# States carried through DRAM with three transfers in place of sixteen, and the turning of halves put two steps later

## The chip, the cores and the metric

The kernel runs on one core of one Trainium2 chip, as one launch. The metric is the device time of that launch in microseconds (us): the median of three runs. One further execution was taken with the hardware profiler on; every row below is of it.

## The reference, cut to what matters

The input is 16 images of 192 channels by 32 x 32 positions (1024 tokens). Each image goes through three parts, each with a residual: a convolution-like mixing part, a windowed attention, and an expert layer (4 experts, top 2 per token). The change is in the mixing part, whose core is a linear recurrence along the rows and along the columns, in both directions, with a state of 16 numbers:

```python
def _ssm1d(x, a_logit, U, V, Win, bin_, Wg, bg, Wout, bout, Wskip, bskip, reverse):
    if reverse:
        x = x[:, ::-1]
    u = jnp.einsum('nld,sd->nls', x, Win) + bin_
    g = jax.nn.sigmoid(jnp.einsum('nld,sd->nls', x, Wg) + bg)
    a = jax.nn.sigmoid(a_logit)
    A = jnp.diag(a) + (U @ V.T).T
    gu = jnp.swapaxes(g * u, 0, 1)
    def step(h, gu_t):
        h = h @ A + gu_t
        return (h, h)
    _, hs = jax.lax.scan(step, h0, gu)
    ...
yr = _ssm1d(rows, *rp, False) + _ssm1d(rows, *rp, True)
yc = _ssm1d(cols, *cp, False) + _ssm1d(cols, *cp, True)
y = (yr + yc) * 0.25
...
return g * y + (1.0 - g) * x
```

The mixed tokens are then normalised and projected to queries, keys and values for the attention.

## The kernel before, in words

**Order of the whole.** While the experts of image i run, the mixing part of image i+1 is done in between, so that TensorE (PE) always has expert work to put into gaps. `experts(i)` goes through 4 blocks of 512 tokens in 6 chunks each, 24 chunks. A chunk n is `ffn1(n)` (5 matmuls into one PSUM bank), a GELU on ScalarE (ACT, `gelu`, L818), a split of the result into two halves of float16 on VectorE (DVE, `split`, L1057 and L1060), and two chunks later `ffn2(n-2)` on PE (L1528 to L1530). `ffn1(n)` waits for `gelu(n-2)`.

**Steps.** The side work is written as generators (`conv`, `tail`, `rest`, `dispatch`), one of each per engine, and each `yield from til(step_no, k)` says that what follows runs in step k+1. The list `STEPS` says how many steps each chunk makes: (a, b) is a steps between `ffn1` and `ffn2` and b steps after `ffn2`. That split counts on PE alone; ACT does `gelu(n)` and then all a+b steps of the chunk, DVE `split(n)` and then all a+b steps. Before the change chunks 0 to 15 have (1, 1), chunks 16 and 17 (2, 1), and chunks 18 to 23 (2, 2). One step is made ahead of chunk 0. Every engine works its own instructions in order, so an instruction that waits holds up all that stands behind it on that engine. There is no planner: the order is this list and the numbers given to `til`.

**The scan.** PE projects the normalised image (L1388); ACT takes a tanh of the gates (L772); DVE multiplies gates and inputs into `GU` in two halves (row kind L994, column kind L998), each of which adds to `gu_ready`. In `GU` the 16 states lie on 16 partitions and the 32 positions of a line along the free axis. The scan itself (L1404, 14 float32 matmuls on ready-made powers of the recurrence, shown as 28 passes) wants eight positions times 16 states on 128 partitions, in `GUP`. `input_moves` does this rearrangement: the SP queue issues 16 DMAs of 8 KB (L588, 8 for each kind), each from 16 partitions to 16 others. PE runs the scan in step 11 and waits there for all 16 (`gu_moved`). ACT copies the result into `HSP` (L779); `state_moves` brings it back with 16 more DMAs (L596), 8 into `HST` for the rows, which GpSimd (POOL) then permutes (`conv_states`, L687 and L688) and SP places (`state_place`, L600), and 8 straight into `XG` for the columns. The states are wanted in step 28, when the mixing of the eight token tiles (L1446 to L1454) begins. Between these moves the SP queue also loads the experts' weights (`expert`, L623) and tokens (`tokens`, L610).

**The turning of halves.** The eight tiles are mixed in steps 28 to 35; the last two in chunk 16. After a tile, DVE ends the residual (L1021, L1023) and takes statistics; after each four tiles POOL raises the variance to the power -1/2 (L678) and makes the shift (L697). ACT normalises four tiles (`first_norm(k)`, L851), DVE splits them into float16 halves (`first_halves(k)`, L1145 and L1146), and PE turns them (12 transposes, L1463; `xnr_ready` is the wait). When both halves are turned, ACT and DVE copy the windows (L490 to L494), and then PE projects them (`project`, L1487), 18 pieces, one in a step. In the numbers of `til`: `first_norm(1)` 36 on ACT, `first_halves(1)` 37 on DVE, turning 37 and 39 on PE, windows 41 and 42, projections 45; and, in `dispatch`, the prefix sums of the router 36 on PE (L1537), `positions` 38 and `schedule` 39 on DVE.

The lines of this order:

```python
STEPS = [(1, 1) if n < 16 else (2, 1) if n < 18 else (2, 2) for n in range(NSEL * HK)] + [(1, 1)]
...
def experts(i, *side):          # ACT
    step(side, STEPS_AHEAD)
    for n in range(blocks_of(i) * HK):
        gelu(i, *divmod(n, HK))
        step(side, sum(STEPS[n % len(STEPS)]))
```

Images 0 to 2 differ: image 0 is mixed before anything else, image 1 after the attention of image 0, with no experts beside it, and image 2 beside the single block of six chunks of image 1. The other 13 images (3 to 15) are mixed beside 24 chunks.

Of the kernel before, what the change touches and what calls it, by code (L numbers as in the profile page):

```python
# [6 lines left out]
F32 = mybir.dt.float32  # L7
# [44 lines left out]
    x_loaded=16, gn_channel=1, gn_mean=1, gn_spread=1, gn_var=1, gn_eps=1, gn_rstd=1, xg_ready=2, xs_ready=2,  # L52
    proj_done=1, tanh_done=1, gu_ready=2, gu_moved=16 * 2 * KP, scan_done=1, hs_copied=1, hs_rows_moved=16 * KP,
    hs_cols_moved=16 * KP, hs_permuted=1, hs_placed=16, xgT_done=NP, h1_read=NP, mixln_eps=1, mixln_rstd=1, h1_pre=1,
    h1_gelu=1, h1T_done=1, h1T_copied=1, mix_done=NT, mix_tanh=NT, mixed=NT,
# [18 lines left out]
def hybrid_kernel(nc, x, proj_w, y_wa, y_wb, y_scale, eye, gavg, cavg, norm_w, norm_b, g1_wT, g1_b, g2_wT, bias_row,  # L74
                  scan_v, scan_u, scan_a, wqkv, wo, bq, bk, bv, mask, w1, w2, b1, gate_w, gate_b, before, after,
                  consts, tri, out, powers, slots, weights):
    ctx = ExitStack()
    with ctx:
# [333 lines left out]
        def at(name, i, k):  # L412

            return i * PER[name] + k
# [46 lines left out]
        def til(count, k):  # L461

            while count[0] < k:
                count[0] += 1
                yield
# [15 lines left out]
        STEPS_AHEAD = 1  # L481
        STEPS = [(1, 1) if n < 16 else (2, 1) if n < 18 else (2, 2) for n in range(NSEL * HK)] + [(1, 1)]
        GATE_AT, MIX_AT = (15, 16, 18, 19), 27
# [98 lines left out]
        def _(sp):  # L582
            def input_moves(i):
                for kind in range(2):
                    sp.wait_ge(s["gu_ready"], at("gu_ready", i, kind + 1))
                    src = GU[32 * kind:32 * kind + S, :].rearrange("s (c i n) -> s c i n", c=KC, i=KP)
                    for k in range(KP):
                        sp.dma_start(GUP[S * k:S * k + S, kind, :, :], src[:, :, k, :]).then_inc(s["gu_moved"], 16)  # L588

            def state_moves(i):  # L590
                sp.wait_ge(s["hs_copied"], at("hs_copied", i, 1))
                for kind, moved in ((0, s["hs_rows_moved"]), (1, s["hs_cols_moved"])):
                    dst = (HST.rearrange("s (c i) n -> s c i n", i=KP) if kind == 0 else
                           XG[97:113, 1, :].rearrange("s (c i n) -> s c i n", c=KC, i=KP))
                    for k in range(KP):
                        sp.dma_start(dst[:, :, k, :], HSP[S * k:S * k + S, kind, :, :]).then_inc(moved, 16)  # L596

# [77 lines left out]
        def _(pool):  # L675
# [8 lines left out]
            def conv_states(i):  # L684
                pool.wait_ge(s["hs_rows_moved"], at("hs_rows_moved", i, 16 * KP))
                pool.wait_ge(s["xs_ready"], at("xs_ready", i, 2))
                pool.tensor_tensor(PSPARE, PSPARE, PSPARE, ALU.mult)  # L687
                pool.tensor_copy(HST2.rearrange("s (h w) -> s h w", h=GH), HST.rearrange("s w h -> s h w")  # L688
                                 ).then_inc(s["hs_permuted"], 1)
# [72 lines left out]
        def _(act):  # L762
# [12 lines left out]
            def conv(i):  # L775
                step_no = [4 if first(i) else 0]
                yield from til(step_no, 10)
                act.wait_ge(s["scan_done"], at("scan_done", i, 1))
                act.activation(HSP[:].rearrange("p a b c -> p (a b c)"), PSUM[:, 3, 0:2 * KC * GW], ACT.Copy  # L779
                               ).then_inc(s["hs_copied"], 1)  # L780
                yield from til(step_no, 22)
                act.wait_ge(s["h1_pre"], at("h1_pre", i, 1))
                act.activation(H1[:], H1[:], ACT.Gelu).then_inc(s["h1_gelu"], 1)
                yield from til(step_no, 25)
                act.wait_ge(s["h1T_done"], at("h1T_done", i, 1))
                act.activation(H1T[:].rearrange("p a b -> p (a b)"), PSUM[:, 0, 0:256], ACT.Copy
                               ).then_inc(s["h1T_copied"], 1)
                for t in range(NT):
                    yield from til(step_no, MIX_AT + t)
                    act.wait_ge(s["mix_done"], at("mix_done", i, t + 1))  # L790
                    if t >= 2:
                        act.wait_ge(s["mixed"], at("mixed", i, t - 1))
                    act.activation(TM[:, (t % 2) * C:(t % 2 + 1) * C], PSUM[:, t % 2, 0:C], ACT.Tanh, scale=0.5
                                   ).then_inc(s["mix_tanh"], 1)
                    if t == 6:
                        first_norm(i, 0)
                yield from til(step_no, 36)
                first_norm(i, 1)
                yield from til(step_no, 41)
                act.wait_ge(s["xn1T_done"], at("xn1T_done", i, 1))  # L800
                windows(act.copy, 0, 0)
                windows(act.copy, 0, 1)
                yield from til(step_no, 42)
                windows(act.copy, 2, 0)
                windows(act.copy, 2, 1).then_inc(s["win_act"], 1)
                yield from til(step_no, 45)
                for n in range(PIECES):
                    if n % 2 == 0:
                        act.wait_ge(s["piece_done"], at("piece_done", i, n + 1))
                        evacuate_piece(act, n, s["piece_act"])  # L810
                    yield
# [108 lines left out]
        def _(dve):  # L920
# [69 lines left out]
            def conv(i):  # L990
# [46 lines left out]
                first_halves(i, 1)  # L1037
                yield from til(step_no, 41)
                dve.wait_ge(s["xn1T_done"], at("xn1T_done", i, 1))
                dve.memset(XW[:, :, 0, 0:PAD - 1], 0.0)  # L1040
                dve.memset(XW[:, :, NB - 1, T - LAST_KEY:KW], 0.0)
                windows(dve.tensor_copy, 1, 0)
                yield from til(step_no, 42)
                windows(dve.tensor_copy, 1, 1).then_inc(s["win_dve"], 1)
                yield from til(step_no, 45)
                for n in range(PIECES):
# [327 lines left out]
        def _(pe):  # L1374
# [17 lines left out]
            def conv(i):  # L1392
                step_no = [4 if first(i) else 0]
                yield from til(step_no, 10)
                pe.wait_ge(s["gu_ready"], at("gu_ready", i, 2))
                pe.wait_ge(s["gu_moved"], at("gu_moved", i, 16 * 2 * KP))
                if not first(i):
# [35 lines left out]
                for t in range(NT):  # L1433
                    yield from til(step_no, MIX_AT + t)
                    if t == 0:
                        pe.wait_ge(s["h1T_copied"], at("h1T_copied", i, 1))
                        pe.wait_ge(s["hs_copied"], at("hs_copied", i, 1))
                        pe.wait_ge(s["hs_cols_moved"], at("hs_cols_moved", i, 16 * KP))
                        pe.wait_ge(s["hs_placed"], at("hs_placed", i, 16))
# [17 lines left out]
                for k in range(2):  # L1457
                    yield from til(step_no, 37 + 2 * k)
                    pe.wait_ge(s["mixed"], at("mixed", i, NT))
# [5 lines left out]
                    if k == 1:  # L1465
                        mm.then_inc(s["xn1T_done"], 1)
                yield from til(step_no, 45)
                pe.wait_ge(s["win_act"], at("win_act", i, 1))
# [336 lines left out]
```

## Time and profile before

| what | us |
|---|---|
| median of three runs | 3132.28 |
| lowest and highest of them | 3127.65, 3137.54 |
| the profiled execution, its own time | 3132.16 |
| its span, first to last instruction | 3130.4 |

The profiled execution lies within the three runs, so its rows can be held against the median. Times in the rows are microseconds from the start of the span. In a timeline each row is a start, a length, the engine, the line of the kernel, the operation with output and input, how many instructions the row merges, and, in brackets, how long the engine sat idle before it and who ended that. "SPq" and "ACTq" are DMA issues on a queue. PEclk is the clock that TensorE was granted, as a share of full speed.

### The profile page before, as it was taken

To read this page: it belongs to the slowest core of one execution; us is meant where nothing else is said; L and a number is where in the kernel's file an instruction comes from. 1 tells how busy PE (TensorE), PEld (TensorE's weight loads), DVE (VectorE), ACT (ScalarE), POOL (GpSimd) and SP (SyncE) were. 2 spreads that over 40 slices of the span, in tenths; PEclk is the share of its full clock that TensorE was granted. 3 is DMA by queue.
4 is the path that set the end of the run, shared out by engine and by line. 5 is a ranking of instruction groups with operands and counts; after the bars stand their busy time and mean duration, and the time that the engine had idled before them with its cause. 6 is when DMAs were issued, how large, how long until landed. Compare 5 with 4: busy or idle time off the path is not lost. (4 is left out here: it accounts for less than half of the span.)

```text
span 3130.4 us, 50074 instructions
## 1 busy us (share of the span) xinstructions
PE 2541.2 (81%) x18177; PEld 1957.0 (63%) x18177; DVE 1945.5 (62%) x5667; ACT 989.8 (32%) x2341; POOL 919.4 (29%) x704
## 2 busy tenths in 40 slices
PE   1367787888888888888888898888888898888597
PEld 0256565666767666675767676676767676676365
DVE  4465655666666656666666657666666666666364
ACT  0031323243342424233342424233342424243122
POOL 0001203051332415051332414151332415051544
PEclk9786878898998989898998989898998989899799
DMA  2520203123242414123242514223242414223565
GB/s 43 118 88 15 58 15 99 36 67 77 67 98 62 110 43 116 49 56 88 66 99 62 110 36 120 52 61 83 65 100 62 110 39 117 53 58 98 132 154 113
DMA packets 272437, 242.20 MB, mean 77 GB/s; under 512 B 208989, under 2 KB 250175, under 8 KB 261569
## 3 DMA queue, kind: packets, MB, share of 16 engines
q1 hardware_dynamic: 211456, 147.61, 17.8%
q0 software_dynamic: 50880, 52.59, 9.5%
q10 hardware_dynamic: 9856, 38.80, 4.0%
q8 instruction: 146, 2.39, 0.3%
q14 instruction: 99, 0.80, 0.1%
HBM read 133.73 MB, written 73.59 MB: 66 GB/s over the span
## 5 line engine op out<-in xcount | busy, mean ns | idle before, releaser
L1510 PE MATMUL PSUM<-XT,WB 128*128 128x512 f16 x2010 | 546.6, 408 | 29.1 <-DMA META<-slots 27.3
L818 ACT ACTIVATE HF<-PSUM,WB 128x512 f32<-128x512 f32 x402 | 277.2, 690 | 692.2 <-PE PSUM L1510 691.4
L678 POOL TENSOR_TENSOR TR<-TV,MHALF 128x4 f32<-128x4 f32 x64 | 75.8, 1185 | 1182.9 <-DVE TV L932 1182.9
L726 POOL DMA_INDIRECT out_dram<-Y,META x228 | 355.7, 1560 | 208.2 <-issue 207.9
L1057 DVE TENSOR_SCALAR HHI<-HF 128x512 f16<-128x512 f32 x402 | 175.6, 437 | 387.1 <-ACT HF L818 385.2
L841 ACT ACTIVATE PSPT<-PSUM,NMX 94x126 f32<-94x126 f32 x1056 | 286.9, 362 | 406.7 <-PE PSUM L1569 288.2
L1528 PE MATMUL PSUM<-WB,HHI 128*128 128x192 f16 x1608 | 413.7, 257 | 0.2
L1529 PE MATMUL PSUM<-WB,HHI 128*128 128x192 f16 x1608 | 412.7, 257 | 0.0
L1530 PE MATMUL PSUM<-WB,HLO 128*128 128x192 f16 x1608 | 412.3, 256 | 0.0
L1510 PEld LDWEIGHTS PSUM<-XT,WB 128*128 128x128 f16 x2010 | 206.8, 107 | 210.5 <-issue 50.8
L1579 PE MATMUL PSUM<-VW,PSPT 126*94 126x33 f32 x2112 | 218.2, 255 | 111.0 <-DVE PSPT L1095 110.9
L1557 PE MATMUL PSUM<-KBD,QT 128*94 128x378 f32 x704 | 296.4, 504 | 14.5 <-ACT PSPT L841 12.8
L711 POOL DMA_INDIRECT slots<-XROW,IDX x256 | 255.3, 997 | 167.4 <-DVE IDX L1253 88.7
L1060 DVE SCALAR_TENSOR_TENSOR HLO<-HF,HHI 128x512 f16<-128x512 f32 x402 | 279.3, 695 | 13.8
L1579 PEld LDWEIGHTS PSUM<-VW,PSPT 126*94 126x94 f32 x2112 | 198.1, 169 | 143.0 <-DVE PSPT L1095 143.0
L1111 DVE TENSOR_REDUCE NMX<-PSUM 94x3 f32<-94x378 f32 x352 | 184.7, 542 | 74.3 <-PE PSUM L1560 72.2
L1487 PE MATMUL PSUM<-OSX,WQKV 128*96 128x372 f16 (+3 forms) x960 | 188.0, 343 | 31.7 <-issue 22.3
L1529 PEld LDWEIGHTS PSUM<-WB,HHI 128*128 128x128 f16 x1608 | 165.3, 103 | 34.6 <-issue 12.2
L1528 PEld LDWEIGHTS PSUM<-WB,HHI 128*128 128x128 f16 x1608 | 168.6, 105 | 27.4 <-issue 7.5
L1404 PE MATMUL PSUM<-GUP,SCAN 128*128 128x64 f32 (+3 forms) x448 | 98.5, 415 | 92.6 <-issue 75.7
L1487 PEld LDWEIGHTS PSUM<-OSX,WQKV 128*96 128x96 f16 x960 | 117.2, 126 | 85.3 <-issue 24.9
L1530 PEld LDWEIGHTS PSUM<-WB,HLO 128*128 128x128 f16 x1608 | 164.9, 103 | 1.4
(270 smaller groups left out, 4393.0 us busy)
## 6 DMA issues: line engine op xcount, KB each, us to landing
WB<-weights SPq DMA_DIRECT2D x67, 1600.0 KB, 7.2
XR<-in_x ACTq DMA_DIRECT2D x16, 768.0 KB, 5.6
out_dram<-X ACTq DMA_DIRECT2D x32, 384.0 KB, 2.4
weights<-WB ACTq DMA_DIRECT2D x4, 1600.0 KB, 6.6
GUP<-TGU SPq DMA_DIRECT2D x256, 8.0 KB, 1.8
slots<-XROW,IDX POOLq DMA_INDIRECT x256, 2.4
out_dram<-Y,META POOLq DMA_INDIRECT x228
HF<-in_w ACTq DMA_DIRECT2D x6, 384.0 KB, 6.3
```

The lines of the kernel that those rows point to most:

```text
L711: pool.indirect_dma_start(slots[:, :].bitcast(I32), bass.IndirectOffsetOnAxis(IDX[:, k, t:t + 1], 0), XROW[:, t, :].bitcast(I32), None, bo ...
L726: pool.indirect_dma_start(out[:, :], bass.IndirectOffsetOnAxis(row, 0), Y[:, wslot(i, j), q, :], None, bounds_check=B * T + BS - 1, oob_is ...
L818: act.activation(HF[:, k % 2, :], PSUM[:, 4 + k % 2, :], ACT.Gelu, scale=1 / (X_UP * W_UP), bias=bias).then_inc(f["gelu_done"], 1)
L841: e = act.activation(PS[0:QS, n % 2, h, :], PSUM[0:QS, n % 2, h * KS:(h + 1) * KS], ACT.Exp, bias=NMX[:, b, n % 2, h:h + 1])
L1060: dve.scalar_tensor_tensor(HLO[:, k % 3, :], HF[:, k % 2, :], H_UP, HHI[:, k % 3, :], ALU.mult, ALU.subtract).then_inc(f["hl_ready"], 1)
L1487: mm = pe.matmul(PSUM[0:HC, n % 4, 0:width], WQKV[:, kind, m, oh * HC:(oh + 1) * HC], XW[:, c, b0:b1, keys], start=(m == 0), stop=(m == 4))
L1510: mm = pe.matmul(dst, WB[:, ws, w:w + 128], XT[:, xs, chunk, :], start=(n == 0), stop=(n == 4))
L1528: pe.matmul(dst, HHI[:, k % 3, tok], w2h, start=False, stop=False, skip_group_check=True)
L1529: pe.matmul(dst, HHI[:, k % 3, tok], w2l, start=False, stop=False, skip_group_check=True)
L1530: mm = pe.matmul(dst, HLO[:, k % 3, tok], w2h, start=False, stop=(k == HK - 1), skip_group_check=True)
L1557: pe.matmul(PSUM[0:QS, n % 2, 0:HH * KS], QT[:, oh, b, :], KBD[:, oh, b, :, :].rearrange("p h k -> p (h k)"), start=True, stop=False)
L1579: mm = pe.matmul(PSUM[0:QS, 2, O_COL + c:O_COL + c + VC], PT[:, n % 2, h, :], VW[:, b, c:c + VC], start=True, stop=True)
```

## The change

- `input_moves`: the two kinds of `GU` are each stored into a new DRAM tensor `states` with one DMA, already in the order of `GUP` (runs of 128 bytes on both sides); when both have landed, one DMA loads `GUP` whole.
- `state_moves`: `HSP` is stored whole with one DMA; when it has landed, one DMA for each kind loads it into `HST` and `XG` (runs of 128 bytes).
- The SP queue gets waits for these stores, and for the loads of the image before.
- `STEPS` gives chunks 16 and 17 four steps as (2, 2). The steps from the 41st on are renumbered by two (windows 43 and 44, projections 47), and so is the turning on PE (39 and 41). `first_norm(1)`, `first_halves(1)` and the steps of `dispatch` keep their numbers.

```diff
-        STEPS = [(1, 1) if n < 16 else (2, 1) if n < 18 else (2, 2) for n in range(NSEL * HK)] + [(1, 1)]
+        STEPS = [(1, 1) if n < 16 else (2, 2) for n in range(NSEL * HK)] + [(1, 1)]
...
             def input_moves(i):
+                if not first(i):
+                    sp.wait_ge(s["gu_moved"], at("gu_moved", i, 0))
                 for kind in range(2):
                     sp.wait_ge(s["gu_ready"], at("gu_ready", i, kind + 1))
-                    src = GU[32 * kind:32 * kind + S, :].rearrange("s (c i n) -> s c i n", c=KC, i=KP)
-                    for k in range(KP):
-                        sp.dma_start(GUP[S * k:S * k + S, kind, :, :], src[:, :, k, :]).then_inc(s["gu_moved"], 16)
+                    sp.dma_start(states[0, kind].rearrange("(k s) (c n) -> s c k n", s=S, n=GW),
+                                 GU[32 * kind:32 * kind + S, :].rearrange("s (c k n) -> s c k n", c=KC, k=KP)
+                                 ).then_inc(s["gu_stored"], 16)
+                sp.wait_ge(s["gu_stored"], at("gu_stored", i, 32))
+                sp.dma_start(GUP[:].rearrange("p a c n -> p a (c n)"), states[0].rearrange("a p f -> p a f")
+                             ).then_inc(s["gu_moved"], 16)
 
             def state_moves(i):
+                if not first(i):
+                    sp.wait_ge(s["hs_rows_moved"], at("hs_rows_moved", i, 0))
+                    sp.wait_ge(s["hs_cols_moved"], at("hs_cols_moved", i, 0))
                 sp.wait_ge(s["hs_copied"], at("hs_copied", i, 1))
+                sp.dma_start(states[1].rearrange("a p f -> p a f"), HSP[:].rearrange("p a c n -> p a (c n)")
+                             ).then_inc(s["hs_stored"], 16)
+                sp.wait_ge(s["hs_stored"], at("hs_stored", i, 16))
                 for kind, moved in ((0, s["hs_rows_moved"]), (1, s["hs_cols_moved"])):
-                    dst = (HST.rearrange("s (c i) n -> s c i n", i=KP) if kind == 0 else
-                           XG[97:113, 1, :].rearrange("s (c i n) -> s c i n", c=KC, i=KP))
-                    for k in range(KP):
-                        sp.dma_start(dst[:, :, k, :], HSP[S * k:S * k + S, kind, :, :]).then_inc(moved, 16)
+                    dst = (HST.rearrange("s (c k) n -> s c k n", k=KP) if kind == 0 else
+                           XG[97:113, 1, :].rearrange("s (c k n) -> s c k n", c=KC, k=KP))
+                    sp.dma_start(dst, states[1, kind].rearrange("(k s) (c n) -> s c k n", s=S, n=GW)).then_inc(moved, 16)
...
# ACT and DVE, conv: windows and projections
-                yield from til(step_no, 41)
+                yield from til(step_no, 43)
...
-                yield from til(step_no, 42)
+                yield from til(step_no, 44)
...
-                yield from til(step_no, 45)
+                yield from til(step_no, 47)
...
# PE, conv: turning, then projections (45 to 47)
-                    yield from til(step_no, 37 + 2 * k)
+                    yield from til(step_no, 39 + 2 * k)
```

The increments that the waits for `gu_moved`, `hs_rows_moved` and `hs_cols_moved` count to go down to 16 each, since each is now one DMA.

## Rows read from the trace of the kernel before

**Rows 1.** The page: busy time (share of the span) and instructions of each engine.

```profile
PE 2541.2 (81%) x18177; PEld 1957.0 (63%) x18177; DVE 1945.5 (62%) x5667; ACT 989.8 (32%) x2341; POOL 919.4 (29%) x704
```

**Rows 2.** The waits of PE: engine, line, releaser: total us, times, longest us.

```profile
PE PSUM L1404 <- issue: 75.7, 15, 9.0
PE PSUM L1463 <- DVE X L1146: 57.7, 28, 4.7
...
PE PSUM L1404 <- DMA GUP<-TGU: 16.8, 1, 16.8
```

**Rows 3.** The timeline around one scan, that of image 9.

```profile
1642.98 10.33 SPq L588 DMA_DIRECT2D GUP<-TGU  x16
1642.98 1.22 DVE L998 SCALAR_TENSOR_TENSOR TGU<-TGU,PSUM 16x1024 f32<-16x1024 f32 x1
...
1646.88 0.35 ACTq L825 DMA_DIRECT2D out_dram<-X  x1
...
1649.98 0.25 PE L1530 MATMUL PSUM<-WB,HLO 128*128 128x192 f16 x1
...
1654.58 6.15 PE L1404 MATMUL PSUM<-GUP,SCAN 128*128 128x128 f32 x28 [4.36 <-issue]
1654.78 0.16 DVE L1299 TENSOR_TENSOR QT<-OC,BV 96x2 f32<-96x2 f32 x1
...
1671.78 0.33 PE L1418 MATMUL PSUM<-EYE,XG 96*128 96x96 f32 x2
```

**Rows 4.** Windows: us, busy of PE, PEld, DVE, ACT, POOL, PEclk, DMA share, GB/s.

```profile
1652.00:1654.00 2.00, 0.00 (x0) 0.00 (x0) 1.97 (x4) 0.00 (x0) 0.00 (x0) 0.51 0.09 13
...
1664.00:1666.00 2.00, 2.00 (x11) 1.97 (x10) 0.75 (x2) 0.00 (x0) 0.00 (x0) 0.58 0.08 12
1666.00:1668.00 2.00, 2.00 (x14) 1.82 (x14) 0.55 (x1) 0.00 (x0) 0.00 (x0) 1.00 0.09 12
```

**Rows 5.** DMA issues by line: count, KB each, median us from issue to landing.

```profile
out_dram<-X ACTq DMA_DIRECT2D x32, 384.0 KB, 2.4
...
GUP<-TGU SPq DMA_DIRECT2D x256, 8.0 KB, 1.8
...
slots<-X SPq DMA_DIRECT2D x4, 400.0 KB, 3.4
...
META<-slots SPq DMA_DIRECT2D x67, 10.0 KB, 2.8
```

**Rows 6.** L265, SCAN<-powers, DRAM to SBUF, 16 times 56 KB in 64-byte runs.

```profile
DMA to landing us min/median/max: 3.2/5.8/5.9
```

**Rows 7.** The timeline around the turning of image 9.

```profile
1721.97 0.19 PE L1537 MATMUL PSUM<-WINB,TRIB 128*128 128x32 bf16 x1
...
1722.17 0.69 ACT L818 ACTIVATE HF<-PSUM,WB 128x512 f32<-128x512 f32 x1 [1.04 <-PE PSUM L1510]
...
1724.50 0.42 DVE L1057 TENSOR_SCALAR HHI<-HF 128x512 f16<-128x512 f32 x1
1724.54 0.44 POOL L697 TENSOR_TENSOR NMR<-NMR,TR 128x4 f32<-128x4 f32 x1
1724.73 0.83 PE L1463 MATMUL PSUM<-EYEH,X 128*128 128x128 f16 x12 [2.39 <-DVE X L1146]
1724.96 0.69 DVE L1060 SCALAR_TENSOR_TENSOR HLO<-HF,HHI 128x512 f16<-128x512 f32 x1
1725.01 1.86 ACT L851 ACTIVATE XN<-X,NMR,TR 128x192 f32<-128x192 f32 x4 [2.15 <-POOL NMR L697]
...
1726.90 0.56 DVE L1145 TENSOR_SCALAR X<-XN 128x768 f16<-128x768 f32 x1 [1.25 <-ACT XN L851]
...
1728.60 0.83 PE L1463 MATMUL PSUM<-EYEH,X 128*128 128x128 f16 x12 [0.97 <-DVE X L1146]
...
1734.20 1.77 PE L1487 MATMUL PSUM<-OSX,WQKV 128*96 128x372 f16 x10 [1.71 <-issue]
```

**Rows 8.** The window from the second halves to the first projection, columns as in rows 4.

```profile
1727.00:1734.00 7.00, 4.52 (x44) 3.20 (x42) 6.46 (x34) 4.13 (x10) 2.89 (x3) 1.00 0.08 29
```

More of the change, by code:

```diff
@@ L52 @@
     x_loaded=16, gn_channel=1, gn_mean=1, gn_spread=1, gn_var=1, gn_eps=1, gn_rstd=1, xg_ready=2, xs_ready=2,
-    proj_done=1, tanh_done=1, gu_ready=2, gu_moved=16 * 2 * KP, scan_done=1, hs_copied=1, hs_rows_moved=16 * KP,
-    hs_cols_moved=16 * KP, hs_permuted=1, hs_placed=16, xgT_done=NP, h1_read=NP, mixln_eps=1, mixln_rstd=1, h1_pre=1,
+    proj_done=1, tanh_done=1, gu_ready=2, gu_stored=16 * 2, gu_moved=16, hs_stored=16, scan_done=1, hs_copied=1, hs_rows_moved=16,
+    hs_cols_moved=16, hs_permuted=1, hs_placed=16, xgT_done=NP, h1_read=NP, mixln_eps=1, mixln_rstd=1, h1_pre=1,
     h1_gelu=1, h1T_done=1, h1T_copied=1, mix_done=NT, mix_tanh=NT, mixed=NT,
@@ L75, in hybrid_kernel @@
                   scan_v, scan_u, scan_a, wqkv, wo, bq, bk, bv, mask, w1, w2, b1, gate_w, gate_b, before, after,
-                  consts, tri, out, powers, slots, weights):
+                  consts, tri, out, powers, slots, weights, states):
     ctx = ExitStack()
@@ L684, in conv_states @@
             def conv_states(i):
-                pool.wait_ge(s["hs_rows_moved"], at("hs_rows_moved", i, 16 * KP))
+                pool.wait_ge(s["hs_rows_moved"], at("hs_rows_moved", i, 16))
                 pool.wait_ge(s["xs_ready"], at("xs_ready", i, 2))
@@ L1037, in conv @@
                 first_halves(i, 1)
-                yield from til(step_no, 41)
+                yield from til(step_no, 43)
                 dve.wait_ge(s["xn1T_done"], at("xn1T_done", i, 1))
@@ L1042, in conv @@
                 windows(dve.tensor_copy, 1, 0)
-                yield from til(step_no, 42)
+                yield from til(step_no, 44)
                 windows(dve.tensor_copy, 1, 1).then_inc(s["win_dve"], 1)
-                yield from til(step_no, 45)
+                yield from til(step_no, 47)
                 for n in range(PIECES):
@@ L1395, in conv @@
                 pe.wait_ge(s["gu_ready"], at("gu_ready", i, 2))
-                pe.wait_ge(s["gu_moved"], at("gu_moved", i, 16 * 2 * KP))
+                pe.wait_ge(s["gu_moved"], at("gu_moved", i, 16))
                 if not first(i):
@@ L1437, in conv @@
                         pe.wait_ge(s["hs_copied"], at("hs_copied", i, 1))
-                        pe.wait_ge(s["hs_cols_moved"], at("hs_cols_moved", i, 16 * KP))
+                        pe.wait_ge(s["hs_cols_moved"], at("hs_cols_moved", i, 16))
                         pe.wait_ge(s["hs_placed"], at("hs_placed", i, 16))
@@ L1466, in conv @@
                         mm.then_inc(s["xn1T_done"], 1)
-                yield from til(step_no, 45)
+                yield from til(step_no, 47)
                 pe.wait_ge(s["win_act"], at("win_act", i, 1))
@@ L1799 @@
     weights = nc.dram_tensor("weights", (E * 128, WROW // 2), I32, kind="Internal").ap()
+    states = nc.dram_tensor("states", (2, 2, 128, KC * GW), F32, kind="Internal").ap()
     powers = nc.dram_tensor("powers", (2 * S, 63, 2 * S), F32, kind="Internal").ap()
-    hybrid_kernel(nc, **aps, out=out, powers=powers, slots=slots, weights=weights)
+    hybrid_kernel(nc, **aps, out=out, powers=powers, slots=slots, weights=weights, states=states)
     res = run(nc, [{"in_" + k: v for k, v in ins.items()}], core_ids=[0])
```

## The prediction, made before the changed kernel ran

> **What bounds the kernel now.** I read the page first: PE is busy 81% of the span, the next engine (DVE) 62% [rows 1]. So the end moves when PE has less to do, waits less, or is clocked higher, in the stretches that repeat for every image. The waits of PE come next. Two of them belong to the change: the scan L1404 waits 75.7 us in 15 images ("issue" there is the wait for the SP queue's transfers) and 16.8 us in image 0; the turning L1463 waits 57.7 us, 28 times [rows 2]. Then the timeline of one image shows each wait in place. Image 9 stands for the 13 images 3 to 15, whose rows repeat this pattern; images 0 to 2 are taken apart.
>
> The scan [rows 3]: DVE gives the first half of the gated inputs at 1642.98 and the second at 1644.20. SP issues 16 transfers for 10.33 us, 0.65 us each; the last lands 1.8 us after its issue [rows 5]. PE ends its expert work at 1650.23, sits idle 4.36 us and starts the scan at 1654.58. The issues are the limit, not the bytes. The idle time costs twice: the granted clock is already down to 0.51 in 1652 to 1654, that is at 1.2 GHz, and comes back to 2.4 GHz only within 1664 to 1666 (0.58, then 1.00) [rows 4]. From 1654.58 to about 1665.7, where 0.58 of that window puts the rise, PE is busy throughout, at half speed.
>
> The turning [rows 7]: PE waits 2.39 us for the first halves and 0.97 us for the second, then 1.71 us for the windows before the first projection at 1734.20. The clock stays up there.
>
> **The change, part by part.**
>
> *The way of the inputs.* Removed: 16 issues, 10.33 us. Added: two stores and, after both have landed, one load. The second store can be issued at 1644.25. No row shows a 64 KB store in 128-byte runs, so I bound it: stores to DRAM land in 2.4 us (384 KB) to 3.4 us (400 KB); I take 2.9, the middle, as this one is smaller but cut finer. The load of 128 KB: 2.8 us is the median of the small META load [rows 5]; SCAN, cut into 64-byte runs, took 3.2 us at best and 5.8 us with others queued before it [rows 6]. A transfer between SBUF partitions takes 1.8 us [rows 5], which nothing here undercuts. I take 2.5 for the load: one DMA, runs of 512 bytes. With 0.1 us for SP to wake up, 2.9 + 0.1 + 2.5 = 5.5 us, bounds 1.8 + 0.1 + 1.8 = 3.7 and 5.8 + 0.1 + 5.8 = 11.7. The scan's inputs are there at 1649.75. PE is free at 1650.23. One thing can be in the way: ACT's store of 384 KB is issued at 1646.88 [rows 3], on the same engines as the load. I allow it 0.6 us and leave a wait of 0.4 us.
>
> A page of the Trainium skill speaks against this step. The Trainium skill, DMA: Bandwidth & Descriptors, Anatomy of one DMA, puts about 2.0 us of fixed cost on each DMA, most of it the receipt of the write, heaviest for DRAM; its Specifications add that runs under 512 bytes are read, modified and written. By its formula two DMAs in a row make an estimate of 2 x 2.0 us + 0.45 us for 192 KB = 4.45 us, without the short runs, and by that no wait would be left: 0.4 us more gained per image. The trace agrees that DRAM is the slower target (2.4 to 3.4 us against 1.8); no run shows the short runs yet.
>
> The gain per image: 75.7 us less the longest, 9.0 of image 1, are 66.7 us in 14 images, 4.8 each [rows 2]. With 0.4 left, 4.4 us. The clock: 11.1 us at half speed become 5.5 us at full speed, if a wait of 0.4 us does not bring it down. I take 5.2, because only one image was read window by window. Together 9.6 us. What is late next? The outputs of the attention need DVE's L1299, ended at 1654.94 [rows 3]; with the scan over by about 1653.7 and two pieces of expert work (some 2 us) behind it, PE comes there at about 1655.7. Nothing stands until the gates L1418, now at 1671.78.
>
> *The way back.* It is costed at nothing. 16 issues of the same kind take 10 us; a store and two loads take some 6 us to the last landing, at 2.9 and 2.5 us as above, so SP is free sooner for the weights behind them. The states are wanted only in step 28, 17 steps after the scan. That cover gone, their 6 us would stand on the path. POOL stands behind the row half as before.
>
> *The turning.* In chunks nothing from the 41st step on moves: old step 42 and new step 44 are both the first b step of chunk 18, and the projections still begin in chunk 19 after ffn2. What moves is (1) the first turning, from before ffn2(15) to behind it; (2) the prefix sums, whose step 37 now lies at the end of chunk 16, ahead of ffn1(17); (3) on ACT, first_norm(1), whose step 37 goes from chunk 17 to chunk 16, so from behind gelu(17) to ahead of it; (4) on DVE, schedule, from behind split(18) to ahead of it. (1) fills the 2.39 us: the prefix sums, at 1721.97 today, wait for the last tile without the ffn1(17) that now fills 1 us ahead of them; then ffn1(17) and ffn2(15) bring PE to the first turning at about 1724.5, so some 0.3 us is left.
>
> (3) is the new wait. first_norm(1) waits for POOL's shift, done at 1724.98, and ends at 1726.87. Today gelu(17) is done at 1722.86, in ACT's idle time, and DVE splits chunk 17 from 1724.50 to 1725.65 while ACT normalises [rows 7]. After the change gelu(17) stands behind first_norm(1): it ends at 1726.87 + 0.69 = 1727.56. split(17), 1.15 us, ends at 1728.75, and only then come the second halves, which today start at 1726.90: 1.85 us later. From there to the first projection DVE is busy 6.46 of 7.00 us [rows 8], and the same pieces are still to do; (4) only changes their order. So the second turning goes from 1728.60 to 1730.45, with PE idle since about 1726.5 (3.9 us), and the first projection from 1734.20 to 1736.05. The loss is 1.85 us, plus an estimate of 0.55 us for images where 3.9 us of idling brings the clock down as the 4.36 us before the scan does. 2.4 us per image; the bounds are a gain of 3.0 (all of 2.39 and 0.97 but 0.4) and a loss of 4.
>
> *Images 0 to 2.* Their inputs come by the same way: 11.6 us from the first issue become 1.25 + 5.5 = 6.75. Image 0 gains 4.5 us of its 16.8 (its weight loads stand behind the scan on ACT, so it is on the path), image 1 4.5, image 2 4.0 and some 3 us of clock. Together 16. The turning there has no experts between and keeps its order.
>
> **The sum.** 13 x (9.6 - 2.4) = 94, plus 16, makes 110 us. The profiled execution took 3132.2 us, the median of the runs is 3132.3, so it can be taken from either: 3022 us. Its own range is 2995 (the turning costs nothing: 13 x 9.6 + 16 = 141, less a few) to 3050 (a wait of 1.5 us left, half the clock's gain).
>
> **The rivals.**
>
> *The clock stays down.* For: the scan's neighbours on PE are small pieces, and a little idling among them may suffice. Against: the 2.39 us before the first turning do not bring it down in image 9 [rows 7, 8]. Then 13 x (4.4 - 2.4) + 12 = 38: 3094 us.
>
> *The turning gains.* If ACT's new order cost nothing, 3.0 of the 3.36 us would go: 13 x (9.6 + 3.0) + 16 = 180: 2952 us. Against it stands the order on ACT, which the diff leaves at 36.
>
> *Two landings in a row take longer than the sixteen issues; slower.* Sixteen issues bring the inputs 11.6 us after the first. Store and load match that at 10.3 us together, and with the turning's loss it decides from some 9 us. At 5.8 us each, SCAN's median [rows 6], the scan starts 1.4 us later than now: 13 x (1.4 + 2.4) = 49: 3181 us. The Trainium skill's rule on runs under 512 bytes (DMA: Bandwidth & Descriptors, Specifications) points this way. Against: SCAN's 5.8 us had other transfers of its own kind queued before it; here the queue is empty.
>
> *The gain is lost again* in a later wait, for POOL's powers or for tokens: 3132 us. Little speaks for it: they follow PE's own progress.
>
> **How the numbers follow.** The forecast gets 0.66, the clock 0.15, the turning's gain 0.08, the slower case 0.07, the lost gain 0.04. The range 2975 to 3096 leaves out the second and third rival, the lost gain's case and the far edges of the forecast. A change within 0.3% (9 us) can't be told from none in this kernel: faster 0.89, same 0.04, slower 0.07.
>
> **What would show it.** Right: L1404 with under 1 us of idle time before it and PEclk 1.00 through the scan; on ACT, L851 of the second tiles ahead of the GELU of chunk 17; L1463 first with almost no wait and then with nearly 4 us; some 7 us less from scan to scan. Wrong: stores or loads of `states` that land after 4 us or more; PEclk 0.50 in the scan although the wait is short; a wait of under 1 us at the second turning.

## The result, and the profile after

The changed kernel takes 3014.2 us (median of 4 runs, 2999.7 to 3016.8) against 3134.9 us before on the same chip (4 runs, 3127.7 to 3139.5). The ratio is 0.9607, 95% interval 0.9571 to 0.9644: some 121 us less, where 110 were forecast. The profiled execution, the longest of the four, took 3016.8 us with a span of 3015.0. In the changed file all lines from the scan's neighbourhood on are 10 further down: the scan is L1414, the turning L1473, the first projection L1497.

The page's first line of the changed kernel, to be read beside [rows 1]:

```profile
PE 2489.6 (83%) x18177; PEld 1904.5 (63%) x18177; DVE 1943.6 (64%) x5667; ACT 986.6 (33%) x2341; POOL 918.5 (30%) x704
```

PE runs the same 18177 instructions in 51.6 us less busy time. Nothing in its work has changed, so this is the granted clock. The rest of the span, in which PE does nothing, went from 589.2 to 525.4 us. The gain is thus 64 us of waiting and 52 us of clock, and this way of splitting a span serves for all the runs below.

The waits of PE, against [rows 2]; three more of the kernel before, for the attention, the first projection and the prefix sums, stand first:

```profile
PE PSUM L1579 <- DVE PSPT L1095: 110.9, 175, 2.3
...
PE PSUM L1487 <- issue: 22.3, 13, 1.7
...
PE PSUM L1537 <- DVE X L1023: 3.8, 2, 1.9
```

```profile
PE PSUM L1473 <- DVE X L1156: 65.2, 32, 4.7
...
PE PSUM L1547 <- DVE X L1033: 15.7, 15, 1.9
PE PSUM L1497 <- issue: 14.1, 13, 1.9
...
PE PSUM L1414 <- DMA GUP<-states: 12.3, 1, 12.3
PE PSUM L1414 <- issue: 7.3, 8, 3.9
```

The scan's 75.7 us in 15 images have become 7.3 us in 8, and 3.9 of these are image 1. The turning's wait has grown by 7.5 us, and the prefix sums (L1547), which waited 3.8 us in 2 images before, now wait in 15. The first projection (L1497) waits less, 14.1 us in place of 22.3.

The timeline around the scan of image 9, against [rows 3]:

```profile
1578.10 1.21 DVE L1008 SCALAR_TENSOR_TENSOR TGU<-TGU,PSUM 16x1024 f32<-16x1024 f32 x1
1578.16 1.76 SPq L588 DMA_DIRECT2D states<-TGU  x2
...
1581.99 0.38 SPq L592 DMA_DIRECT2D GUP<-states  x1
1581.99 0.41 ACTq L835 DMA_DIRECT2D out_dram<-X  x1
...
1585.09 0.25 PE L1540 MATMUL PSUM<-WB,HLO 128*128 128x192 f16 x1
...
1585.37 3.28 PE L1414 MATMUL PSUM<-GUP,SCAN 128*128 128x128 f32 x28
```

The inputs need 7.21 us from the first issue to the start of the scan (11.6 before), and PE goes from expert work into the scan without a gap. The 28 passes of the scan take 3.28 us instead of 6.15. The windows say why (columns as in [rows 4]): PEclk is 1.00 where it was 0.51.

```profile
1584.00:1586.00 2.00, 1.97 (x31) 1.74 (x30) 1.79 (x6) 0.50 (x2) 0.96 (x1) 1.00 0.33 121
1586.00:1588.00 2.00, 2.00 (x21) 2.00 (x19) 1.93 (x5) 0.00 (x0) 0.00 (x0) 1.00 0.03 8
```

The DMA issues of the changed kernel, against [rows 5]:

```profile
out_dram<-X ACTq DMA_DIRECT2D x32, 384.0 KB, 3.0
...
states<-TGU SPq DMA_DIRECT2D x32, 64.0 KB, 2.7
GUP<-states SPq DMA_DIRECT2D x16, 128.0 KB, 3.4
states<-HSP SPq DMA_DIRECT2D x16, 128.0 KB, 1.8
```

And the timeline around the turning of image 9, against [rows 7]:

```profile
1647.02 0.19 PE L1547 MATMUL PSUM<-WINB,TRIB 128*128 128x32 bf16 x1 [0.91 <-DVE X L1033]
...
1649.59 0.20 POOL L707 TENSOR_TENSOR NMR<-NMR,TR 128x4 f32<-128x4 f32 x1
...
1649.79 0.83 PE L1473 MATMUL PSUM<-EYEH,X 128*128 128x128 f16 x12 [0.30 <-DVE X L1156]
1649.83 1.86 ACT L861 ACTIVATE XN<-X,NMR,TR 128x192 f32<-128x192 f32 x4 [3.63 <-POOL NMR L707]
1651.59 1.24 ACT L828 ACTIVATE HF<-PSUM,WB 128x512 f32<-128x512 f32 x2
1652.29 0.43 DVE L1067 TENSOR_SCALAR HHI<-HF 128x512 f16<-128x512 f32 x1 [2.65 <-ACT HF L828]
1653.36 0.55 DVE L1155 TENSOR_SCALAR X<-XN 128x768 f16<-128x768 f32 x1
...
1655.05 0.83 PE L1473 MATMUL PSUM<-EYEH,X 128*128 128x128 f16 x12 [3.35 <-DVE X L1156]
```

ACT sits idle for 3.63 us in front of the second tiles' norm (L861) and only then does the GELU of chunk 17 (L828, two of them together). DVE waits for that, and PE behind DVE: 3.35 us of idle time before the second turning, where the kernel before had 0.97.

In image 9 the clock does not fall there, as the windows show:

```profile
1652.00:1654.00 2.00, 0.00 (x0) 0.00 (x0) 1.64 (x4) 0.83 (x2) 0.00 (x0) 1.00 0.00 0
...
1656.00:1658.00 2.00, 2.00 (x19) 1.41 (x17) 1.69 (x12) 2.00 (x5) 1.06 (x1) 1.00 0.00 0
```

But image 9 does not stand for all. In image 10, behind the same 3.35 us, the clock is at half from about 1823.8 to 1827.2, and the same 12 transposes take 1.26 us in place of 0.83:

```profile
1823.58 1.26 PE L1473 MATMUL PSUM<-EYEH,X 128*128 128x128 f16 x12 [3.35 <-DVE X L1156]
```

```profile
1824.00:1826.00 2.00, 2.00 (x17) 1.90 (x16) 1.73 (x14) 1.12 (x2) 0.53 (x1) 0.50 0.00 0
1826.00:1828.00 2.00, 2.00 (x11) 1.12 (x10) 1.80 (x9) 1.78 (x7) 1.52 (x2) 0.69 0.14 51
```

So it goes at the second turning of images 4, 6, 8, 10, 12, 14 and 15 in this profile, at some 1.7 us each (half of what runs at half speed); in images 3, 5, 7, 9, 11 and 13 the clock stays up behind the same wait.

### The profile page after: what moved, and what is told of

The parts are those of the page before. It is cut to its first block and busy times, and to the rows that moved or that the text cites. A ratio compares the mean times of both kernels' runs of the same rounds, so it can differ in the third digit from the quotient of the medians.

```text
span 3015.0 us, 49688 instructions
## 1 busy us (share of the span) xinstructions
PE 2489.6 (83%) x18177; PEld 1904.5 (63%) x18177; DVE 1943.6 (64%) x5667; ACT 986.6 (33%) x2341; POOL 918.5 (30%) x704
## 3 DMA queue, kind: packets, MB, share of 16 engines
q8 instruction: 146, 2.39, 0.3%
## 5 line engine op out<-in xcount | busy, mean ns | idle before, releaser
L1520 PE MATMUL PSUM<-XT,WB 128*128 128x512 f16 x2010 | 538.5, 403 | 28.6 <-DMA META<-slots 27.2
L828 ACT ACTIVATE HF<-PSUM,WB 128x512 f32<-128x512 f32 x402 | 274.7, 687 | 636.4 <-PE PSUM L1520 629.7
L1538 PE MATMUL PSUM<-WB,HHI 128*128 128x192 f16 x1608 | 408.2, 254 | 0.2
L1539 PE MATMUL PSUM<-WB,HHI 128*128 128x192 f16 x1608 | 407.1, 253 | 0.0
L1497 PE MATMUL PSUM<-OSX,WQKV 128*96 128x372 f16 (+3 forms) x960 | 186.9, 342 | 24.8 <-issue 14.1
L1497 PEld LDWEIGHTS PSUM<-OSX,WQKV 128*96 128x96 f16 x960 | 116.7, 126 | 78.2 <-issue 21.3
L1105 DVE COPY PSPT<-PSUM 126x282 f32<-126x282 f32 x352 | 141.2, 439 | 3.3 <-PE PSUM L1579 3.2
```

Of the source, the lines that this page charges most:

```text
L828: act.activation(HF[:, k % 2, :], PSUM[:, 4 + k % 2, :], ACT.Gelu, scale=1 / (X_UP * W_UP), bias=bias).then_inc(f["gelu_done"], 1)
L1497: mm = pe.matmul(PSUM[0:HC, n % 4, 0:width], WQKV[:, kind, m, oh * HC:(oh + 1) * HC], XW[:, c, b0:b1, keys], start=(m == 0), stop=(m == 4))
L1520: mm = pe.matmul(dst, WB[:, ws, w:w + 128], XT[:, xs, chunk, :], start=(n == 0), stop=(n == 4))
L1538: pe.matmul(dst, HHI[:, k % 3, tok], w2h, start=False, stop=False, skip_group_check=True)
L1539: pe.matmul(dst, HHI[:, k % 3, tok], w2l, start=False, stop=False, skip_group_check=True)
```

## The experiments

All ratios are to the kernel before, run on the same chip. The last two columns are of the profiled execution, which is not always a middle one (the longest of its kernel's runs for the changed kernel, e1, e2, e4 and e6, the shortest for e5): PE's busy time (the clock, since the 18177 instructions are the same, but for the filler in e5, 15 times some 4.16 us) and the rest of the span.

| kernel | median us | ratio, 95% interval | PE busy | rest |
|---|---|---|---|---|
| before | 3130 to 3135 | 1 | 2541.2 | 589.2 |
| changed | 3014.2 | 0.9607 [0.9571, 0.9644] | 2489.6 | 525.4 |
| e1, transfers only | 2978.9 | 0.9508 [0.9490, 0.9527] | 2468.1 | 513.5 |
| e2, steps only | 3175.0 | 1.0122 [1.0086, 1.0157] | 2594.5 | 587.6 |
| e5, before with filler | 3046.5 | 0.9721 [0.9701, 0.9741] | 2513.4 (some 62 filler) | 527.1 |
| e6, loaded twice | 3093.9 | 0.9865 [0.9845, 0.9886] | 2540.1 | 553.5 |
| e4, inputs only | 3008.4 | 0.9609 [0.9590, 0.9628] | 2503.0 | 519.8 |
| e3, GELU first | 2991.4 | 0.9548 [0.9512, 0.9585] | 2472.9 | 516.7 |
| e7, order mended | 2977.9 | 0.9494 [0.9470, 0.9518] | 2475.0 | 495.5 |
| e9, late plan | 2981.2 | 0.9535 [0.9503, 0.9567] | 2477.7 | 491.5 |
| e8, old steps, late plan | 2963.7 | 0.9481 [0.9457, 0.9504] | 2464.6 | 491.6 |

**Transfers only** (e1: the changed kernel with the steps of before).

```diff
-STEPS = [(1, 1) if n < 16 else (2, 2) for n in range(NSEL * HK)] + [(1, 1)]
+STEPS = [(1, 1) if n < 16 else (2, 1) if n < 18 else (2, 2) for n in range(NSEL * HK)] + [(1, 1)]
...
-yield from til(step_no, 43)     # and 44, 47, 39 + 2 * k
+yield from til(step_no, 41)     # and 42, 45, 37 + 2 * k
```

> The three transfers, with the steps of before. My account (the new order on ACT costs 1.85 to 2.4 us an image in 13 images): 24 to 31 us faster than the changed kernel, about 2985 us, ratio to before 0.952. Rival (the later turning gains 2 to 3 us an image): about 3045 us, ratio 0.971.

Measured: 0.9508, 151.5 us less, where the prediction's terms for the transfers give 13 x 9.6 + 16 = 141. PE's busy time falls by 73.1 us and the rest of the span by 75.7, nearly half and half, as in the prediction (5.2 of clock and 4.4 of waiting per image). The scan waits 5.7 us in 4 images, beside the 12.1 of image 0.

**Steps only** (e2: the kernel before with the new steps).

```diff
-STEPS = [(1, 1) if n < 16 else (2, 1) if n < 18 else (2, 2) for n in range(NSEL * HK)] + [(1, 1)]
+STEPS = [(1, 1) if n < 16 else (2, 2) for n in range(NSEL * HK)] + [(1, 1)]
...
-yield from til(step_no, 41)     # and 42, 45, 37 + 2 * k
+yield from til(step_no, 43)     # and 44, 47, 39 + 2 * k
```

> The new steps alone, with the sixteen transfers of before. My account: 24 to 31 us slower than before, ratio 1.008 to 1.010, PE idle over 3 us ahead of the second turning. Rival (the later turning gains): ratio 0.988.

Measured: 1.0122, some 38 us more by the ratio and 44.7 by the medians. The steps cost time by themselves, but not in the way that was expected. The sign that was named is there: PE idles 3.35 us ahead of the second turning in each of images 3 to 15. Yet the rest of the span stays as it was (587.6 against 589.2 us), because other waits shrink by as much as the turning's and the prefix sums' grow (7.5 and 11.9 us): the first projection's from 22.3 to 9.5 us and, in the attention, that of L1579 from 110.9 to 103.2.

```profile
PE PSUM L1579 <- DVE PSPT L1095: 103.2, 158, 2.9
...
PE PSUM L1487 <- issue: 9.5, 13, 2.0
```

PE's busy time is 53.3 us up instead. Two windows of this kernel, of 21 us each, both in the attention, 118 us behind the scan of image 7 (1323.21) and 123 us behind that of image 8 (1497.87):

```profile
1441.00:1462.00 21.00, 18.35 (x138) 13.68 (x139) 13.10 (x44) 8.98 (x34) 6.89 (x5) 1.00 0.65 113
1621.00:1642.00 21.00, 20.77 (x79) 14.04 (x78) 8.96 (x28) 4.87 (x18) 6.91 (x5) 0.51 0.58 90
```

In the second the granted clock is 0.51, that is 1.2 GHz, throughout, although PE is busy 20.77 of 21 us, and it gets through 79 instructions in place of 138. The profile of this kernel has five such stretches. Four of them lie between the scans of images 3 to 15: those intervals from scan to scan take 186.3 to 187.6 us, the eight without one 174.7 to 181.4, 176.8 in the mean, where the kernel before has 176.5. So a stretch costs some 10 us; the fifth lies behind the scan of image 2, whose interval is 5.7 us longer than before. Together they are some 45 of the 53. Most of the rest lies at the turnings: the clock falls at the second turning of ten images (all of 3 to 15 but 9, 11 and 13), where in the kernel before it falls at the first turning of four (8, 11, 13 and 15); six more at 1.7 us make 10.

**The clock by itself** (e5: the kernel before, with 25 matmuls of no use in front of the wait for the transfers, from image 1 on; they write a bank that is free there).

```diff
 pe.wait_ge(s["gu_ready"], at("gu_ready", i, 2))
-pe.wait_ge(s["gu_moved"], at("gu_moved", i, 16 * 2 * KP))
 if not first(i):
     pe.wait_ge(s["x2_ready"], at("x2_ready", i - 1, 2))
+    keep_busy(25, 3)
+pe.wait_ge(s["gu_moved"], at("gu_moved", i, 16 * 2 * KP))
```

> The kernel before with 25 idle matmuls (128 by 378, bfloat16, into a PSUM bank that is free then) on PE in images 1 to 15, between the last expert work and the wait for the sixteen transfers; the wait itself is as long as before. My account (the clock is half of the gain): the scan runs at PEclk 1.00 and the kernel gains 13 to 14 times 5.2 = 65 to 73 us, ratio 0.977 to 0.979. Rival (the clock matters little, the gain is the wait): ratio 0.995 to 1.000.

Measured: 0.9721, 88.1 us less, with the sixteen transfers and their time as they were. The timeline of image 9 and its windows (columns as in [rows 4]):

```profile
1597.88 4.16 PE L1547 MATMUL PSUM<-MASKB,ONESB 128*128 128x378 bf16 x25
1602.35 3.31 PE L1405 MATMUL PSUM<-GUP,SCAN 128*128 128x128 f32 x28 [0.30 <-DMA GUP<-TGU]
```

```profile
1600.00:1602.00 2.00, 2.00 (x13) 1.04 (x11) 1.97 (x4) 0.00 (x0) 0.00 (x0) 1.00 0.09 13
1602.00:1604.00 2.00, 1.70 (x16) 1.65 (x15) 1.83 (x9) 0.00 (x0) 0.00 (x0) 1.00 0.00 0
```

The filler stands where PE idled, the clock stays at 1.00, and the scan takes 3.31 us. The 88.1 us are 5.9 per image, more than was expected, but not all of them are the scan's. In the stretches from 12 to 35 us behind the scans of images 3 to 15 the mean PEclk is 0.95 here and 0.90 both in the kernel before and in e1, which is an estimate of 17 us (13 x 23 us x 0.057). Without them it is 4.7 per image, about as much as the idling itself (4.8).

**A longer way through DRAM** (e6: the changed kernel with the load made twice, the second behind the landing of the first).

```diff
 sp.wait_ge(s["gu_stored"], at("gu_stored", i, 32))
+sp.dma_start(GUP[:].rearrange("p a c n -> p a (c n)"), states[0].rearrange("a p f -> p a f")
+             ).then_inc(s["gu_twice"], 16)
+sp.wait_ge(s["gu_twice"], at("gu_twice", i, 16))
 sp.dma_start(GUP[:].rearrange("p a c n -> p a (c n)"), states[0].rearrange("a p f -> p a f")
```

> The changed kernel with the load of the inputs done twice, one after the other: the chain is one landing longer, 2.1 to 3.4 us, and no SBUF work changes. My account: a wait of about 2.5 us comes back; 14 times 2.5 = 35 us if the clock stays up at such a wait (ratio 0.972), 35 + 14 times 5 = 105 us if it falls (ratio 0.994). Rival (the chain has room to spare): same as the changed kernel, ratio 0.961.

Measured: 0.9865, some 80 us more than the changed kernel, between the two cases. One more landing of 2.1 us brings back a wait of 2.0 to 3.6 us in images 2 to 15 and, with it, the slow clock: of the 78.6 us between the two spans, 50.5 are PE's busy time. The wait, and the windows around the scan of image 9, which starts at 1631.67:

```profile
PE PSUM L1417 <- issue: 37.6, 15, 6.1
```

```profile
1630.00:1632.00 2.00, 0.33 (x3) 0.36 (x4) 1.93 (x6) 0.00 (x0) 0.00 (x0) 1.00 0.22 66
1632.00:1634.00 2.00, 2.00 (x15) 2.00 (x14) 1.93 (x5) 0.00 (x0) 0.00 (x0) 0.64 0.04 8
1634.00:1636.00 2.00, 2.00 (x11) 2.00 (x11) 1.90 (x6) 0.00 (x0) 0.00 (x0) 0.50 0.00 0
```

The change has little to spare here: 2 us more on the way cost two thirds of its gain. The two loads also part a load by itself from one in company (each time from issue to landing, min/median/max, first load and second):

```profile
DMA to landing us min/median/max: 2.1/3.3/4.8
```

```profile
DMA to landing us min/median/max: 2.0/2.1/2.3
```

From image 2 on the first is issued in the same instant as ACT's store of 384 KB, the second 3 us or more later. Image 1 of the changed kernel speaks for the company and against the place in the order: there ACT's store is issued 1.9 us earlier, and the only load lands in 2.1 us.

**The way back** (e4: the changed kernel with `state_moves` as before, 16 transfers between SBUF partitions).

```diff
-sp.dma_start(states[1].rearrange("a p f -> p a f"), HSP[:].rearrange("p a c n -> p a (c n)")
-             ).then_inc(s["hs_stored"], 16)
-sp.wait_ge(s["hs_stored"], at("hs_stored", i, 16))
 for kind, moved in ((0, s["hs_rows_moved"]), (1, s["hs_cols_moved"])):
...
-    sp.dma_start(dst, states[1, kind].rearrange("(k s) (c n) -> s c k n", s=S, n=GW)).then_inc(moved, 16)
+    for k in range(KP):
+        sp.dma_start(dst[:, :, k, :], HSP[S * k:S * k + S, kind, :, :]).then_inc(moved, 16)
```

> The changed kernel, but the scanned states go back with the sixteen transfers of before; only the gated inputs go through DRAM. My account (the way back is hidden): same as the changed kernel within 6 us, ratio 0.961. Rival (a freer SP queue and earlier states are part of the gain): 15 us or more slower than the changed kernel, ratio 0.966 or more.

Measured: 0.9609, against 0.9607 for the whole change. The second half of the change is worth nothing that can be measured; its cover of 17 steps holds with either way.

**GELU first** (e3: the changed kernel with ACT's `first_norm(1)` one step later, behind the GELU of chunk 17).

```diff
-yield from til(step_no, 36)
+yield from til(step_no, 37)
 first_norm(i, 1)
```

> The changed kernel with first_norm(1) on ACT one step later, so that the GELU of chunk 17 comes ahead of it again; nothing else is touched. My account: the second turning comes 1.85 us sooner, 13 times 1.85 = 24 us, about 2990 us, ratio 0.954. Rival (the loss at the second turning lies in DVE's schedule or in POOL's shift, not in ACT's order): same as the changed kernel, ratio 0.961.

Measured: 0.9548, some 18 us less than the changed kernel by the ratios, whose intervals just overlap. The turning's wait goes from 65.2 to 47.1 us, and the second turning of image 9 waits 1.96 us in place of 3.35. But the first projection then waits 24.5 us in place of 14.1, so only 8.7 us leave the rest of the span; PE's busy time falls by 16.7. At the second turning, which now waits 1.96 us in images 3 to 15, the clock falls in image 4 alone, where it fell in seven images of the changed kernel.

**The order mended, and its parts** (e7: e3 with the prefix sums also a step later, and DVE's planning of the experts, `schedule`, behind the copies of the windows; e9: the same without moving the prefix sums; e8: the transfers only, with the planning behind the copies).

```diff
-yield from til(step_no, 39)
+yield from til(step_no, 46)     # 44 with the old steps (e8)
 schedule(i, ...)
...
-yield from til(step_no, 36)     # e7 only, ahead of the prefix sums on PE
+yield from til(step_no, 37)
```

> The changed kernel with first_norm(1) one step later on ACT, the prefix sums one step later on PE (behind ffn1 of chunk 17), and DVE's schedule behind the windows (step 47). My account: besides the 24 us of the first, DVE reaches the windows 2.4 us sooner and the 1.9 us ahead of the first projection go: 13 times 3.6 = 47 us less than the changed kernel, about 2967 us, ratio 0.946. Rival (another wait, for ACT's windows or for the tokens of the next image, takes the place): about 2990 us, ratio 0.954.

> The transfers of the change with the old steps, and DVE's planning of the experts (schedule) put behind the copies of the windows, four steps later than it stood. With the old steps the first projection waits 22.4 us in 13 images (1.72 each), and in the planning's 2.4 us just ahead of the last window copy lies the reason. If that is so, that wait goes and next to nothing takes its place: some 2979 - 20 = 2958 us, 0.945 of before (0.942 to 0.948), and below the version with the mended new steps (0.9494). Rival: the copies on ACT end as late as those on DVE, or the plan is now late for the experts: 2975 to 2985, 0.951.

> The changed kernel with the GELU of chunk 17 back ahead of the second tiles' first norm, and the planning behind the window copies, but the prefix sums left where the change puts them, at the end of chunk 16. Its only difference from the mended order is the place of the prefix sums. The wait for the second halves summed to 47.1 us with them there and to 61.1 us with them in chunk 17. If that difference counts, this run is 14 us below the mended order: 2964 us, 0.945 (0.942 to 0.948). Rival: the prefix sums' own wait (15.7 us in 15 images), which the mended order does not have, eats it: 2978, 0.949.

Measured: e7 0.9494, e8 0.9481, e9 0.9535. In all three the first projection's wait for the windows in 13 images is gone from the waits of PE (22.3 us before, 22.4 in e1, 24.5 in e3), and the rest of the span is 21 to 25 us shorter than in e1 (for e8) or e3 (for e7 and e9): the planning, some 2.4 us of DVE's time per image, stood in front of the last copies. That part came as expected. The times came less far down than the waits: e7 lies between its account (0.946) and its rival (0.954), e8 at the upper edge of its account (0.942 to 0.948), and e9 above both its account and its rival (0.949). The runs of e9 go from 2965.8 us at a mean clock of 0.920 to 3002.0 us at 0.906, so what the place of the prefix sums is worth cannot be told from e7 and e9, whose profiles differ by 4 us of waiting. By the ratios e8 is the lowest of all, though its interval overlaps those of e7 and e1; it is 15 us below e1 by the medians, and its runs (2956.9 to 2973.3) don't touch those of e1 (2976.0 to 2983.4, on another chip, where the kernel before has 3130.4 us against 3132.0 beside e8). It beats the changed kernel by 1.3%, and it has none of the new steps.

## Why the prediction was right, point by point

*The way of the inputs* came as worked out: 7.21 us from the first issue to the scan, where 6.75 + 0.6 were forecast. The store took 2.7 us (forecast 2.9). The load took 3.4 (forecast 2.5 + 0.6), but its parts were off: alone it takes 2.1, and the company of ACT's store, which was foreseen at this place, costs some 1.2 rather than 0.6. The two errors cancel, which is luck. The wait that is left was put at 0.4 us; without images 0 and 1 it is 3.4 us in all, 0.24 for each of 14 images.

The landings that decide this are 2.1 us for the load alone, 2.7 for a store of 64 KB in runs of 128 bytes, and 1.8 for the 128 KB store of the way back, in runs of 512 bytes. The Trainium skill, DMA: Bandwidth & Descriptors, Anatomy of one DMA, has a fit for DMAs issued by GpSimd, 2.0 us plus the bytes at 436 GB/s, which taken for the SP queue makes an estimate of 2.3 us for 128 KB and 2.15 for 64 KB. The trace agrees for the load (2.1), less so for the two stores (2.7 for 64 KB, 1.8 for 128 KB). That DRAM is the slower target, which the prediction read from 2.4 to 3.4 us against 1.8, came from transfers of unlike size: the 128 KB store to DRAM lands in 1.8 us, like 8 KB between SBUF partitions. The Trainium skill, DMA: Bandwidth & Descriptors, Specifications, says that runs under 512 bytes are read, modified and written. The trace agrees so far that the store in 128-byte runs is the slower one, by some 0.9 us; the two stores also differ in the partitions that they read (16 and 128), which no run takes apart. In any case 2.7 us is far from the landings of 5.8 us that the slower rival needed.

*The clock* was put at 5.2 us per image; e1 shows 73.1 us less busy time, 4.9 for each of 15 images, and e5 5.9 where the clock alone is mended, some 4.7 of them around the scan. The rival in which it stays down is out: PEclk is 1.00 in the first 4 us of the scans of images 2 to 15 but one, that of image 5, which waits 1.60 us behind a load of 4.9 us and has 0.65. But e6 shows how near it was: with 2 us more on the way PEclk is 0.50 in the scan.

*The way back* costs nothing and brings nothing, as e4 shows.

*Images 0 to 2* were put at 16 us. The scan of image 3 starts 28.8 us earlier than before (564.90 against 593.72), of which some 5 are its own wait: 24. The term was 8 us too small, and both halves of that are clock: from the scan of image 2 to that of image 3 PE's busy time falls by 7 us (126.6 to 119.2), where 3 were taken, and from the scan of image 1 to that of image 2 by 4 (122.9 to 118.9), where the sum has none.

*The rate* was put at 7.2 us per image. From the scan of image 3 to that of image 15 the lead grows from 28.8 to 112.75 us (2598.90 against 2711.65), that is 84 in 12 images: 7.0.

*The turning* is the step that was right in sum and wrong in its parts. Forecast were 2.4 us of loss per image, 31 in all; the changed kernel's ratio lies 0.0099 above that of e1, which is 31 us, give or take 13 by the two intervals. The mechanism on ACT stands in the rows as it was described: the second norm ahead of the GELU, PE idle 0.3 us before the first turning (forecast 0.3) and 3.35 before the second (forecast 3.9). What failed is the size of both terms in "The loss is 1.85 us, plus an estimate of 0.55 us". In waiting, the rest of the span is 11.9 us longer than in e1, 0.9 per image: the prefix sums' wait of 0.91 us was seen but not counted, while the first projection's wait fell from 22.4 us in e1 to 14.1 in sum, so that it does not come 1.85 later in each image. In clock, PE's busy time is 21.5 us up, 1.7 per image, and the term of 0.55 covers the smaller part of it. At the turnings the clock falls in seven of the 13 images (the second turning), where in e1 it falls in four (the first turning of images 3, 5, 8 and 14, behind 2.39 us): three more, some 5 us, 0.4 per image, near the estimate. Some 3 us more are the scan of image 5. The rest, some 12 us, which no term has, lies behind the turnings, above all in the attention behind the scan of image 8: 1527 to 1548, of the same kind as the five stretches of e2, where the interval to the next scan is 176.7 us and the neighbours' are 168.2. The line of that window:

```profile
1527.00:1548.00 21.00, 20.78 (x82) 14.22 (x82) 8.93 (x28) 4.87 (x18) 6.73 (x5) 0.52 0.56 90
```

So 0.9 and 1.7 us stand where 1.85 and 0.55 were forecast, and that the sum came out is luck. And e2's loss, 38 to 45 us where 24 to 31 were expected, is clock nearly alone.

That image 9 stands for the 13 is what hid the clock at the turnings. Already in the kernel before, the 2.39 us ahead of the first turning bring it down in images 8, 11, 13 and 15, so "The clock stays up there" holds for image 9 and others, not for all.

That the new steps of the change lower the clock shows in every run and not only in the profiles: the mean clocks are 0.879 to 0.888 in the four runs of e2 against 0.890 to 0.896 in the 27 of the kernel before that were run beside the experiments, and 0.916 to 0.919 in the changed kernel against 0.921 to 0.923 in e1. In the changed kernel it is ACT's order, with its wait of 3.35 us, that does it: in e3, whose only difference is this order, they are 0.920 to 0.925, and from 85 to 135 us behind the scans of images 3 to 15 the clock of e3's profile does not fall at all. It is not the only thing that can: one run of e9, which has e3's order, comes down to 0.906. What makes it stay down for 21 us is open. The stretches lie some 120 us behind a scan, in work that the steps don't move. Behind the scans of image 3 and later, the profiles with the old steps (before, e1, e5, e8) have none, and of those with the new ones e2 has four, e4 two, the changed kernel, e6 and e7 one each, e3 and e9 none; but behind the scan of image 2, e8 has one too, as have e2, e7 and e9. At this place the clock also goes down in other images and comes back within 4 us, in the kernel before, for one, in images 8, 11 and 13. In the changed kernel these are images 4, 6, 10, 12 and 14; they and image 8 are images in which the clock fell at the second turning as well. In e7 and e8 it goes down there in images without a fall at a turning, so a fall at the turning is not needed for one in the attention.

*The other rivals.* The turning's gain (2952 us) is out by the 3.35 us of the second turning; even e7, with ACT's order mended, stays at 2978. The gain lost again is out by the lead, which grows to the last scan.

In sum: 13 x 7.0 + 24 = 115, the difference of the two spans, against 110. The upper end of the forecast's own range does not follow from its terms: a wait of 1.5 us left and half the clock's gain take 13 x (1.1 + 2.6) = 48 us off the 110, which makes 3070 us and not 3050.

## What to carry to other kernels

Where a transfer stands in front of TensorE, price its idle time twice: once as waiting, and once as the granted clock that the work behind it gets; here the two were about equal (75.7 and 73.1 us in e1), and matmuls of no use in the gap, with no transfer mended, gave 88 us where mending the transfers gave 152. Split a span into PE's busy time at equal instructions and the rest before explaining a difference: it tells a clock from a wait in one line. Look at the same place in every repetition before one of them stands for all: image 9 shows no loss of clock at the turning, image 10 does. And take a change of several parts apart: of the three here, the transfers in gave all of it, the transfers back nothing, and the new steps took a fifth of it back.

## What the runs showed of the hardware that was not expected

- The granted clock can stay at 1.2 GHz for 21 us while PE is busy 99% of the time (20.77 of 21.00 us in e2, 20.78 in the changed kernel), at a place where in e2 it is 2.4 GHz in the image before with PE busy for 18.35 of 21. One such stretch costs some 10 us, and runs of one kernel (e9) spread over 36 us with mean clocks from 0.906 to 0.920.
- The length of a gap alone does not tell whether the clock falls: 2.15 us without work ahead of the scan are followed by 0.50 (e6, image 9), 3.35 us ahead of the second turning by 1.00 (changed kernel, image 9), and the same 3.35 us before the same work one image later by 0.50 (image 10).
- Sixteen small transfers between SBUF partitions, at 0.65 us of issue each, are slower than three through DRAM whose landings lie in series, 2.7 and 3.4 us.
- A load of 128 KB from DRAM lands in 2.1 us alone and in 3.3 us when a store of 384 KB from another queue is issued with it.
